# Expert rows by a plain load, turned on TensorE, instead of a transposing load

## The reference, cut to what matters

```python
# layer 0: E, TOP_K = 16, 4, F = 512
hidden = gelu(einsum('bld,efd->blef', x, w1) + b1)
exp_out = einsum('blef,edf->bled', hidden, w2) + b2
fused = sum(softmax(topv)[..., None] * take(exp_out, topi), axis=2)
# layer 1: NUM_EXPERTS = 8, TOP_K = 2, HIDDEN = 512
h = silu(x @ Wg[e]) * (x @ Wu[e])
out = sum over the 2 experts of combine * (h @ Wd[e]) * 12 ** -0.5
```

## Time and profile before

| | |
|---|---|
| median of 3 runs | 1382.13 us (1377.95 to 1402.3) |
| profiled execution, device time | 1396.11 us |
| its span | 1394.2 us |
| busy: PE, DVE, ACT, POOL | 966.7, 802.0, 547.5, 631.3 us |
| expert tiles of layer 0, first to last matmul | 606.60 to 914.99 us |
| expert tiles of layer 1, first to last matmul | 1171.39 to 1326.28 us |

### The profile page before, as it was taken

How to read it: one execution, slowest core, us unless ns; L and a number is a source line. 1 busy time by engine, 2 the same in 40 slices (tenths; PEclk the granted TensorE clock), 3 DMA queues, 4 the chain that set the end, 5 groups by cost and what they waited for, 6 DMA issues and landing times.

```text
span 1394.2 us, 32331 instructions
## 1 busy us (share of the span) xinstructions
PE 966.7 (69%) x9696; PEld 694.2 (50%) x9767; DVE 802.0 (58%) x2366; ACT 547.5 (39%) x1318; POOL 631.3 (45%) x629
## 2 busy tenths in 40 slices
PE   4999989888898995058887777735444344999900
PEld 1455555555555553046666666623333233988800
DVE  3567666656766645135555555537567644666656
ACT  2455445444444433034444444411222122665600
POOL 2123254636454546635555554523555643555421
PEclk9779586767767655579999999966567666999965
DMA  4000011101011111232222222231223113222232
GB/s 140 16 17 24 17 37 30 43 22 43 27 40 32 36 34 40 84 67 61 55 59 62 58 63 63 61 98 65 72 69 111 62 38 81 64 59 53 47 108 83
DMA packets 133078, 78.13 MB, mean 56 GB/s; under 512 B 101666, under 2 KB 114121, under 8 KB 132992
## 3 DMA queue, kind: packets, MB, share of 16 engines
q1 hardware_dynamic: 119104, 50.35, 14.6%
q0 software_dynamic: 13312, 25.31, 5.7%
q10 hardware_dynamic: 576, 1.34, 0.3%
HBM read 31.71 MB, written 32.63 MB: 46 GB/s over the span
## 4 chain that ended last, share of the span: by engine, by line
PE 30%; issue 25%; SPq 17%; POOL 14%; DVE 5%; ACT 4%; DMA 3%; POOLq 0%; another core or an unknown queue 0%; ACTq 0%; DVEq 0%
POOL xs L581 8%; SPq L448 6%; SPq L445 5%; PE proj L1301 4%; PE t L1337 3%; SPq L452 2%; PE t L1334 2%; PE s L1321 2%; POOL prob_lo L546 2%; PE t L1332 2%; PE avbank L1501 2%; PE proj L1501 2%; POOL w_lo L606 1%; SPq L404 1%; PE t L1480 1%
## 5 line engine op out<-in xcount | busy, mean ns | idle before, releaser
L628 POOL DMA_INDIRECT yt<-ysb,to_now x224 | 234.7, 1048 | 253.9 <-ACT ysb L1194 151.3
L581 POOL DMA_INDIRECT xs<-x1p,sidx x192 | 189.6, 987 | 57.1 <-issue 51.4
L546 POOL TENSOR_TENSOR prob_lo<-prob,prob_hi 128x384 bf16<-128x384 f32 (+1 forms) x80 | 77.6, 970 | 253.6 <-ACT prob_hi L1124 253.6
L861 DVE CAST h_hi<-act_out 128x512 bf16<-128x512 f32 x152 | 70.5, 464 | 157.8 <-ACT act_out L1207 139.9
L1123 ACT ACTIVATE prob<-t 128x384 f32<-128x384 f32 (+1 forms) x160 | 82.0, 512 | 155.2 <-PE t L1337 125.5
L716 DVE TENSOR_REDUCE nm<-s 128x4 f32<-128x512 f32 x160 | 107.6, 687 | 37.8 <-PE s L1321 36.0
L1480 PE MATMUL s<-xt,w_hi 128*128 128x256 bf16 x296 | 82.9, 280 | 61.7 <-DMA xt<-xs 52.1
L862 DVE TENSOR_TENSOR h_lo<-act_out,h_hi 128x512 bf16<-128x512 f32 x152 | 106.8, 702 | 5.2
L1480 PE MATMUL t<-xt,w_hi 128*128 128x256 bf16 x296 | 82.1, 278 | 20.8 <-DMA xt<-xs 18.2
L1321 PE MATMUL s<-kst,qst 32*128 32x128 bf16 x640 | 76.9, 253 | 17.6 <-issue 11.5
L1501 PE MATMUL avbank<-w_hi,h_hi 128*128 x448 | 82.9, 221 | 6.4 <-issue 4.6
(11 more groups left out here) (216 smaller groups left out, 2754.1 us busy)
## 6 DMA issues: line engine op xcount, KB each, us to landing
w_raw<-w_all SPq DMA_DIRECT2D x56, 256.0 KB
gat<-yt SPq DMA_DIRECT2D x8, 1024.0 KB
gat<-yt SPq DMA_DIRECT2D x8, 512.0 KB, 3.9
yt<-ysb,to_now POOLq DMA_INDIRECT x224
xs<-tail_rows SPq DMA_DIRECT2D x24, 129.0 KB
xs<-x1p,sidx POOLq DMA_INDIRECT x192
out<-ow SPq DMA_DIRECT2D x8, 256.0 KB, 2.3
xt<-xs SPq DMA_TRANSPOSE x112
```

The lines of the kernel that those rows point to most:

```text
L546: pool.tensor_tensor(prob_lo[:, g, 0:width], prob[:, g % 2, 0:width], prob_hi[:, g, 0:width], ALU.subtract).then_inc(low_odd, 1)
L581: pool.indirect_dma_start(out=xs[n][:, :], out_offset=bass.IndirectOffsetOnAxis(sidx[:, par, at:at + 1], 0), in_=x1p[:, par, t, k, :], in_ ...
L628: pool.indirect_dma_start(out=yt[n][:, :], out_offset=bass.IndirectOffsetOnAxis(to_now[:, u, s:s + 1], 0), in_=ysb[:, u, s, :], in_offset= ...
```

## The change

Rows come by a plain DMA into a new buffer `xg` of four slots, 128 x 2 x 258 words each, numbers included. SP reads the table once per group of four and waits, ahead of each load, for `x_turned` and `to_ready` of tile j - 4. PE turns the tile: four transposes of 128 x 128 bf16 into a PSUM bank (`xbank` or `proj[1]` in turn), three tiles ahead of its outputs. DVE copies 512 bf16 columns from there to `xt`, which shrinks from four slots to two, and copies the numbers out of `xg` to `to_now`. In layer 1 the gated values are written in place over `act_out`.

```diff
+        xg = sb("xg", [P, RING, S2, XW], BF16)
+        xt = sb("xt", [P, 2, 2, TILE], BF16)
-        hid = sb("hid", [P, 2, NC_H, TILE])
+        hid = act_out
+        h_bank, y_bank, x_bank = s_bank + t_bank, [avbank, proj[0]], [xbank, proj[1]]
...
 SP, group(g):
+                    rows = rows_of(RING * g, RING)
                     for u in range(RING):
-                        row = row_of(RING * g + u)
                         if not (type(g) is int and g == 0):
-                            sp.wait_ge(h_ready[n], hidden_of * (RING * g + u - RING + 1))
+                            sp.wait_ge(x_turned[n], RING * g + u - RING + 1)
+                            sp.wait_ge(to_ready[n], RING * g + u - RING + 1)
                             apart(sp)
-                        load_rows(row, u)
...
-                        load_numbers(row, slot)
+                        sp.dma_start(xg[:, u, :, :], xs[n][bass.ds(rows[u], TILE), :].rearrange("(s p) d -> p s d", s=S2)
+                                     ).then_inc(xg_loaded[n][u], 16)
...
 DVE:
+                def take_rows(j, u, k):
+                    dve.wait_ge(x_turned[n], j + 1)
+                    if not (type(j) is int and j < 2):
+                        dve.wait_ge(h_ready[n], (NC_H // 2, NC_H)[n] * (j - 1))
+                    dve.tensor_copy(xt[:, u % 2, :, :].rearrange("p h r -> p (h r)"),
+                                    x_bank[u % 2][:, 0:TILE].bitcast(BF16)).then_inc(xt_ready[n], 1)
+                def take_numbers(j, u, k):
+                    dve.wait_ge(xg_loaded[n][u], 16 * k + 16)
+                    if not (type(k) is int and k == 0):
+                        dve.wait_ge(y_stored[n][u], 16 * S2 * k)
+                    dve.tensor_copy(to_now[:, u, :], xg[:, u, :, 2 * D:XW].bitcast(U32).rearrange("p s o -> p (s o)")
+                                    ).then_inc(to_ready[n], 1)
...
 DVE, group(g), at the end of tile j, behind its last subtraction:
+                        take_numbers(j, u, g)
+                        if u < RING - 3 or not last:
+                            take_rows(j + 3, (u + 3) % RING, g)
...
 PE:
+                def turn_rows(j, u, k):
+                    pe.wait_ge(xg_loaded[n][u], 16 * k + 16)
+                    if not (type(j) is int and j < 2):
+                        pe.wait_ge(xt_ready[n], j - 1)
+                    rows = x_bank[u % 2][:, 0:TILE].bitcast(BF16).rearrange("p (h r) -> p h r", h=2)
+                    for h in range(2):
+                        for k in range(S2):
+                            ins = pe.transpose(rows[:, h, k * P:(k + 1) * P], xg[:, u, k, h * D:(h + 1) * D], ident_b)
+                    ins.then_inc(x_turned[n], 1)
...
                         outputs(RING * g + u, u, es[u], last)
+                        ahead = u + LOOK + 1
+                        if ahead < RING or not last:
+                            turn_rows(RING * g + ahead, ahead % RING, g if ahead < RING else g + 1)
                         ahead = u + LOOK
...
 PE, hidden(j):
-                    pe.wait_ge(xt_loaded[n][u], 16 * g + 16)
+                    pe.wait_ge(xt_ready[n], j + 1)
```

More of the change, by code:

```diff
@@ L332, in program @@
          table_ready, table_turned, table_kept, tails_ready, tails_stored,
-         h_ready, act_done, split_done, yp_ready, y_done, tile_step, all_stored) = [
+         h_ready, act_done, split_done, yp_ready, y_done, tile_step, all_stored, sending, x_turned, xt_ready, to_ready) = [
             pair_of(n) for n in (
@@ L336, in program @@
                 "table_ready table_turned table_kept tails_ready tails_stored "
-                "h_ready act_done split_done yp_ready y_done tile_step all_stored").split()]
+                "h_ready act_done split_done yp_ready y_done tile_step all_stored sending x_turned xt_ready to_ready").split()]
         def ring_of(name):
             return [[sem(f"{name}{n}_{u}") for u in range(RING)] for n in range(2)]
-        xt_loaded, to_loaded, y_stored = ring_of("xt_loaded"), ring_of("to_loaded"), ring_of("y_stored")
+        xg_loaded, y_stored = ring_of("xg_loaded"), ring_of("y_stored")
         gathered = [pair_of("gathered0_"), pair_of("gathered1_")]
@@ L441, in expert_tiles, with rows_of @@
             def expert_tiles(n):
[L442 to L454, removed]
+                def rows_of(first, count):
+                    _, values = nc.values_load_multi_w_load_instructions(
+                        table[0:1, bass.ds(first, count)], engines=(mybir.EngineType.SP,), min_val=0,
+                        max_val=experts[n] * REGION - TILE,
+                        skip_runtime_bounds_check_because="the tile table holds rows of this layer's regions")
+                    return values
@@ L473, in expert_tiles @@
-                sp.wait_ge(table_kept[n], 1)
[L474 to L479, removed]
+                        sp.dma_start(xg[:, u, :, :], xs[n][bass.ds(rows[u], TILE), :].rearrange("(s p) d -> p s d", s=S2)
+                                     ).then_inc(xg_loaded[n][u], 16)
@@ L481, in load_outputs @@
+                sp.wait_ge(table_kept[n], 1)
+                over_tiles(sp, n, group)
             def load_outputs(n, b):
@@ L623, in group @@
                     for u in range(RING):
-                        pool.wait_ge(to_loaded[n][u], 16 * g + 16)
+                        pool.wait_ge(to_ready[n], RING * g + u + 1)
                         pool.wait_ge(y_done[n], RING * g + u + 1)
-                        apart(pool)
+                        pool.sem_inc(sending[n], 1)
                         for s in range(S2):
@@ L845, in expert_tiles, with group @@
             def expert_tiles(n):
-                def group(g):
+                def take_rows(j, u, k):
[10 more added lines that the diff above has]
+                                    ).then_inc(to_ready[n], 1)
+                def group(g, last=False):
                     ch = Chain(dve, tile_step[n], 2 * RING * g)
@@ L853, in group @@
                         else:
-                            dve.wait_ge(yp_ready[n], j - 1)
+                            before = j if last and u == 0 else j - 1
+                            dve.wait_ge(yp_ready[n], before)
                             if n == 1:
-                                dve.wait_ge(split_done[n], 2 * j - 2)
+                                dve.wait_ge(split_done[n], 2 * before)
                         if n == 0:
@@ L873, in group @@
                                                   ALU.subtract).then_inc(split_done[n], 1)
+                        take_numbers(j, u, g)
+                        if u < RING - 3 or not last:
+                            take_rows(j + 3, (u + 3) % RING, g)
                 dve.wait_ge(table_kept[n], 1)
-                more = over_tiles(dve, n, group)
-                dve.wait_ge(split_done[n], 2 * RING * more + 2 * RING)
+                for j in range(3):
+                    take_rows(j, j, 0)
+                more = more_groups(dve, n)
+                group(0)
+                with dve.Fori(1, more) as g:
+                    group(g)
+                group(more, last=True)
+                dve.wait_ge(yp_ready[n], RING * more + RING)
                 apart(dve)
@@ L1213, in group @@
                             if not (type(j) is int and j < 2):
-                                act.wait_ge(gated, NC_H * j - NC_H)
+                                act.wait_ge(split_done[n], 2 * j - 2)
                             for c in range(NC_H):
@@ L1479, in hidden_chunk @@
                     w_h, w_l = w_hi[n][:, bass.ds(at, P)], w_lo[n][:, bass.ds(at, P)]
-                    pe.matmul(dst, w_h, xt[:, u, 0, :], start=True, stop=False)
-                    pe.matmul(dst, w_h, xt[:, u, 1, :], start=False, stop=False)
-                    return pe.matmul(dst, w_l, xt[:, u, 0, :], start=False, stop=True)
+                    pe.matmul(dst, w_h, xt[:, u % 2, 0, :], start=True, stop=False)
+                    pe.matmul(dst, w_h, xt[:, u % 2, 1, :], start=False, stop=False)
+                    return pe.matmul(dst, w_l, xt[:, u % 2, 0, :], start=False, stop=True)
                 def outputs(j, u, e, last):
@@ L1531, in expert_tiles @@
                 pe.wait_ge(lo_done, (CHUNKS_0, CHUNKS)[n])
+                for u in range(LOOK + 1):
+                    turn_rows(u, u, 0)
                 for u in range(LOOK):
```

2 lines of the change are left out of this document (removed).

## The result

The changed kernel takes 1487.78 us (median of 4 runs, 1471.34 to 1501.36), the kernel before 1392.22 us beside it (4 runs). The ratio is 1.0657, 95% interval 1.0579 to 1.0735: slower, as forecast, and by about twice the amount (96 us where I had 49). The profiled execution took 1483.5 us.

What follows compares the result with a forecast made beforehand. SP was taken to bound layer 0 and PE layer 1. Layer 0 -5, layer 1 +51 and stage starts +3 gave +49 us: 1445 on the profiled 1396.1, 1439 on the four-run mean of 1390; range 1392 to 1490.

Steps and rivals of the forecast that it cites:

- SP no longer bounds: SP's queue, which bounded layer 0 at 4.06 us a tile, keeps one plain load per tile and bounds nothing.
- PE's pace: Layer 0 per tile if only PE's own work bounded it: 2.77 us before the change, 3.33 with transposes and group heads.
- The ring: DVE's copy of tile j + 3 waits behind outputs(j), so DVE and PE alternate: 3.89 us in layer 0, 5.38 in layer 1.
- Layer 0, -5 forecast: Layer 0's 76 tiles: 3.99 us each, group heads included, against 4.06 before, so -5 us.
- The hop from DVE to PE: Step from DVE's last subtraction to PE's output matmuls, taken as 0.06 us per tile.
- The way from the transposes to the copy: Wake of DVE after PE's transposes, ahead of its copy to xt, taken as 0.10 us per tile.
- Layer 1, +51 forecast: Layer 1's 36 tiles: 5.38 us plus 0.34 for group heads, 5.72 against 4.30 before, so +51 us.
- the clock falls: Rival: PE's pauses in layer 1 drop its clock to 1.2 GHz for a third of the tiles, +50, 1490 us; chance 0.06.
- Start of the stages, +3 forecast: Turns, copies and a plain load ahead of each stage's first product replace one transposing load: 1.5 us twice, +3 us.
- The slow copy: Rival: DVE's copy from PSUM takes 0.68 us, not 0.46; +73 in all, 1463 us; chance 0.15.
- the slow transposes: Rival: PE's four transposes take 1.12 us, 0.73 more in each of 112 tiles, +82, 1521 us; chance 0.07.
- The faster rival: Rival: transposes are ready when DVE wants to copy; layer 0 -55 us, layer 1 +8, 1346 us; chance 0.09.

Runs made afterwards that it cites:

- the quick one: Not a kernel but the chip of one set of runs, on which the kernel before took 1336.6 us and not 1390.
- the later copy: Changed kernel, but DVE copies tile j + 2, not j + 3, at the end of tile j: 1395.32 us, ratio 0.9957 to the kernel before.
- the copy as words: Changed kernel, turned rows copied as 256 four-byte words instead of 512 bf16: 1433.66 us (ratio 1.0711), on another chip 1485.95 us (1.0696).
- the run in which POOL waits: Changed kernel, but in layer 1 POOL scatters tile j only after DVE's copy of tile j + 4, except the last group: 1453.49 us, ratio 1.0428.

## Why the prediction was right, and where its sum was short

The prediction said slower, 1439 us, 1392 to 1490. The mechanism was right in both layers, and several sizes were off. That 1487.78 lies inside the range, by 2 us, is luck: 20 us of the loss came from something that no rival held.

- **SP no longer bounds: right.** 2% of the chain. The load lands in 2.2 us and is never late in the steady state: PE and its weight loads wait for `xg` only at the stages' starts. That layer 0 would otherwise fall to PE's pace did not hold: with SP's table reads by groups alone it took 298.4 us on a chip of this kind, 10 less, and 224.1 on the quick one.
- **The ring: right, shown.** Taking it apart gave back the whole loss (the later copy, ratio 0.9957 against 1.0657), and layer 1 without POOL's hold-up runs at 5.38 us a tile and 207.8 us in all, where 5.38 and 36 x 5.72 = 205.9 were forecast.
- **Layer 0, -5 forecast, +10 measured.** Three terms were too small. "Twelve output matmuls 12 x 0.056 = 0.67 us" was 0.80 from start to start: the row it came from is PE in full flow; here PE starts them after a wait, and the first ones start 0.11 us apart. The hop from DVE to PE was 0.14, not the 0.06 of the earlier trace rows. The way from the transposes to the copy was 0.23 for 0.10, of which 0.1 is TensorE's late signal; on the quick chip it was 0.13, and the tile 4.03 us. The copy took less of the ring, 0.34 us of pitch for 0.46; the transposes took the forecast 0.39. Sum: 3.89 + 0.13 + 0.08 + 0.13 - 0.12 = 4.11, against 4.10 read from the trace.
- **Layer 1, +51 forecast, +82 measured.** The ring was right; the missing 31 us are TensorE's signals held up behind POOL's DMAs and the clock, 29.4 us by experiment. I had costed POOL at nothing, because its waits are long past; that its work might delay another engine's was in no rival. The rival "the clock falls" had the right sign at 0.06 and priced a third of the tiles at double; ten of the 36 tiles lost some 19 matmuls each to half clock, and it cost 9 to 11 us.
- **Start of the stages, +3 forecast:** the first hidden product comes 1.7 and 1.9 us after the first transpose. The windows above begin with the transposes, so this is part of the +10 and the +82. From layer 0's last matmul to layer 1's first hidden product it is 258.0 us for 256.4, the forecast 1.5 more; for layer 0 what lies ahead varies too much to tell.
- **The slow copy and the slow transposes: both out.** The copy takes 0.425 us, the four transposes 0.39. By the Trainium skill, "VectorE: DVE Perf Modes", section "The TRN2 errata", the estimate was 0.39 us; the trace has 0.425, and both my 0.46 and the estimate lie 0.035 us off. The Trainium skill, "TensorE: Matmul & The Clock Gate", part 4, gives about 275 ns for a bf16 transpose; here one lasts 0.22 us and the next starts 0.056 us later, so what counts on the ring is four in 0.39 us.
- **The faster rival ("DVE never waits for PE")** was made real by the later copy, and its price of 1346 us was wrong on that chip: it took PE's rate from matmuls in flow and 0.34 us a tile for the group heads, and layer 0 took 4.01 us a tile, 0.7 above that price, with PE idle where it waits for no semaphore. The earlier trace rows had shown 8.9 us of "issue" in PE's waits; I had not asked what it becomes when PE has no other pause.

## What to carry to other kernels

A copy that one engine makes for another belongs where its source is already finished: placed one tile too near, a copy of 0.4 us costs 0.13 us a tile in one layer and 2.3 in the other, and placing it one tile later took a few lines. Price a matmul block on a ring with its start after a wait (0.80 us for 12, not 0.67). Look at when a semaphore is raised, and not only at when the waiting engine goes on: it tells which of the two is late. Split a change before judging it: the table read by groups was worth 2 to 3% by itself, and the rest of the change buried it.

## What the runs showed of the hardware beyond this

- One engine's work can delay another that shares no semaphore with it: the signals of TensorE's transposes came up to 1.15 us late where POOL's indirect DMA lay over their end, and the copy started about 0.7 us after that DMA's end; with the DMAs moved, no copy was late. It showed in every set of runs but the quick chip's, where none of TensorE's signals was late.
- Chips differ by more than the change: the kernel before took 1387 to 1392 us beside three sets of runs and 1336.6 beside the fourth, and layer 0 of the kernel with the table read by groups took 298.4 and 224.1 us. A kernel bound by a ring (the copy as words: 318.2 and 313.6 us in layer 0) hardly feels it; one bound by TensorE's own stream does. Each set ran on one chip, so chip and occasion are not told apart. Only ratios of kernels measured beside each other are comparable.
- A pause of 2.42 us in PE was followed by 3.8 us at a mean clock of 0.55, and pauses of 2.40 and 2.49 us elsewhere by none. With the pauses of the run in which POOL waits, about 1 us long, the clock stayed at 1.00 from 1180 to 1360 us.
